# Two GNN layers over a binary adjacency: comparisons shared eight and eight, counts one chunk ahead, x first and in eighths

## What is computed

```python
def _L0_gnn_ref(h, adj, W, a, w_ih, w_hh, b_ih, b_hh):
    Wh = h @ W
    src = Wh @ a[:F_out]
    dst = Wh @ a[F_out:]
    e = jax.nn.leaky_relu(src + dst.T, ALPHA)
    att = jnp.where(adj > 0, e, NEG_INF)
    att = jax.nn.softmax(att, axis=1)
    h_prime = att @ Wh
    gi = h_prime @ w_ih.T + b_ih
    gh = h @ w_hh.T + b_hh
    r, z, n = ...            # sigmoid, sigmoid, tanh(i_n + r * h_n)
    return (1.0 - z) * n + z * h

def _L1_gnn_ref(x, adj_matrix, W, b):
    h = jnp.einsum('nd,ed->ne', x, W) + b
    return jnp.matmul(adj_matrix, h)

h = jnp.maximum(_layernorm(x, axis=-1), 0.0)
x = x + _L0_gnn_ref(h, adj, ...)
h = jnp.maximum(_layernorm(x, axis=-1), 0.0)
x = x + _L1_gnn_ref(h, adj, L1_gnn_W, L1_gnn_b)
```

## Time and profile before

| | us |
|---|---|
| median of three runs | 1727.31 (1723.8 to 1727.42) |
| the profiled execution | 1724.32 |
| its span | 1722.4 |

### The profile page before, as it was taken

One profiled execution on the slowest core, in us unless ns is written; L12 is line 12 of the kernel. 1 busy time (PEld: TensorE's weight loads), 2 busy tenths in 40 slices (PEclk: granted clock), 3 DMA queues, 4 the chain that ended last, 5 costly groups with the idle time before them and its releaser, 6 DMA issues.

```text
span 1722.4 us, 35016 instructions
## 1 busy us (share of the span) xinstructions
PE 1571.6 (91%) x13260; PEld 1341.9 (78%) x13260; DVE 1237.2 (72%) x2668; ACT 925.9 (54%) x1419; POOL 34.3 (2%) x57
## 2 busy tenths in 40 slices
PE   3468999999999999899998999999999999999998
PEld 3346777777877878787877887778788888888887
DVE  4898999999999999999999999999925000000000
ACT  4767777777867777776887777777600000000000
POOL 2000000000000000000000000000000000000000
PEclk9678999999999999999999999999999999999999
DMA  7448888887888878888788887888635444444430
GB/s 300 161 162 318 296 304 323 319 313 272 324 321 316 318 270 317 323 321 319 270 324 323 318 319 271 319 326 321 263 150 220 166 164 164 170 172 175 174 137 13
DMA packets 78594, 446.02 MB, mean 259 GB/s; under 512 B 8992, under 2 KB 38624, under 8 KB 57056
## 3 DMA queue, kind: packets, MB, share of 16 engines
q1 hardware_dynamic: 72512, 440.34, 68.3%
q10 hardware_dynamic: 6048, 5.25, 0.9%
HBM read 361.63 MB, written 83.92 MB: 259 GB/s over the span
## 4 chain that ended last, share of the span: by engine, by line
PE 41%; DVE 23%; DMA 14%; issue 12%; ACT 8%; DVEq 1%; ACTq 0%; SPq 0%
PE A L894 26%; DMA X<-in_adjb_dram 14%; PE A L811 11%; DVE M L596 6%; DVE Y L582 5%; DVE M L604 4%; ACT JK L429 3%; ACT M L419 3%; PE GP L834 1%; DVE AE L613 1%; DVE h2n L672 1%; DMA X<-in_L_gnn_a_dram 1%; ACT M L385 1%; PE GP L835 1%; DVE nm L619 1%
## 5 line engine op out<-in xcount | busy, mean ns | idle before, releaser
L811 PE MATMUL A<-TB,M 128*128 128x259 f16 x8192 | 959.1, 279 | 54.2 <-issue 32.4
L811 PEld LDWEIGHTS A<-TB,M 128*128 128x128 fp8e4 x8192 | 806.6, 99 | 195.9 <-issue 60.3
L429 ACT ACTIVATE JK<-X 128x4096 uint8<-128x4096 uint32 x124 | 447.3, 3607 | 1.4 <-DMA X<-in_adjb_dram 1.3
L596 DVE TENSOR_SCALAR M<-SB,nd 128x256 fp8e4<-128x256 f32 x1280 | 347.4, 346 | 4.9 <-issue 4.2
L419 ACT ACTIVATE M<-SB,dsteep 128x256 fp8e4<-128x256 f32 x768 | 319.4, 500 | 0.1
L582 DVE TENSOR_SCALAR Y<-X 128x4096 fp8e4<-128x4096 f32 x128 | 292.6, 2286 | 16.8 <-DMA X<-in_adjb_dram 16.5
L724 DVE SCALAR_TENSOR_TENSOR hp<-A,XT 128x256 f32<-128x256 f32 x32 | 13.6, 424 | 373.1 <-PE A L894 364.6
L894 PE MATMUL A<-WG,X 128*128 128x256 f16 x2048 | 225.5, 273 | 0.9 <-DVE WG L678 0.9
L894 PE MATMUL A<-WG,TB 128*128 128x256 f16 x2048 | 224.9, 273 | 0.0
L894 PEld LDWEIGHTS A<-WG,X 128*128 128x128 fp8e4 x2048 | 200.3, 98 | 24.2 <-DVE WG L678 1.1
L894 PEld LDWEIGHTS A<-WG,TB 128*128 128x128 fp8e4 x2048 | 200.4, 98 | 23.2
(11 more groups left out here) (128 smaller groups left out, 733.5 us busy)
## 6 DMA issues: line engine op xcount, KB each, us to landing
X<-in_adjb_dram SPq DMA_DIRECT2D x128, 2048.0 KB, 8.9
mask_bytes<-Y SPq DMA_DIRECT2D x128, 512.0 KB, 5.6
X<-mask_bytes SPq DMA_DIRECT2D x16, 2048.0 KB, 9.0
TB<-mask_bytes SPq DMA_DIRECT2D x16, 2048.0 KB, 9.3
M<-in_xb_dram SPq DMA_DIRECT2D x4, 1024.0 KB, 8.8
h_columns<-Y SPq DMA_DIRECT2D x16, 256.0 KB, 2.0
h_rows<-M SPq DMA_DIRECT2D x4, 1024.0 KB, 4.2
XT<-in_xb_dram SPq DMA_DIRECT2D x32, 128.0 KB, 8.4
```

What stands on the lines that cost most here:

```text
L429: nc.scalar.activation(to, X[c % 2][:, :].bitcast(u32), ACT.Sign, accum_out=nz[:, bass.ts(g, 1), c:c + 1].rearrange("p g c -> p (g c)")).t ...
L596: ins = nc.vector.tensor_scalar(rows(mask1(c), jj), SB[u][:, :], nd[:, j:j + 1], None, ALU.is_ge, saturate=False)
L811: ins = nc.tensor.matmul(A[t][m][:, 0:2 * TW + 1], rows((mask1, mask2)[m](c), jj)[:, t * P:(t + 1) * P], TB[:, c * JC + jj, m, 0:2 * TW + ...
```

## The change

Eight edits come together.

1. `sign_mask` takes eight tiles of a chunk and `compare` eight, in place of six and ten. In the first row block ScalarE takes all sixteen (`first_on_act`).
2. `count` runs one chunk ahead: after `sign_mask` of chunk c stands the count of chunk c + 1. In the first block it stands where it stood, and the block's end has one more.
3. x is loaded in eight pieces, and SP waits for the last of them before it asks for the first adjacency chunks.
4. The statistics are taken in eighths, one piece ahead of the normalisation. VectorE normalises six tiles of each eight (L541 of the new kernel), ScalarE two. The rectifier moves out of it, into the copy of the transposed tiles (`column`) and into the first operation of `updated`.
5. `features`, the copies into WG, moves from VectorE to ScalarE.
6. `ones_of` of the very first chunk moves ahead of the chain of small operations. The transposed tiles are staged in AE and Y[1], so that Y[0] is free for it.
7. Two one-element activations (Exp, Sigmoid) are put where their function tables should be loaded.
8. Buffers X1, XT, HS, HT become slices of one tile R; semaphores are merged (three `turn` into one, which nobody waits on).

```diff
-ON_ACT = 6
+ON_ACT = 8
+BY_DVE = 6
+        def first_on_act(g):
+            return 0 if isinstance(g, int) and g == 0 else JC - ON_ACT
...
-                for q in range(4):
-                    sp.dma_start(H[:, q * 16:(q + 1) * 16, :], xb[:, q * 16:(q + 1) * 16, :]).then_inc(p_x[q], 16)
+                for q in range(8):
+                    sp.dma_start(H[:, q * 8:(q + 1) * 8, :], xb[:, q * 8:(q + 1) * 8, :]).then_inc(p_x[q], 16)
+                sp.wait_ge(p_x[7], 16)
...
-                    nc.scalar.activation(hTq[k % 4], TP[k % 2][:, :], ACT.Copy).then_inc(p_ht, 1)
+                    nc.scalar.activation(hTq[k % 4], TP[k % 2][:, :], ACT.Relu).then_inc(p_ht, 1)
+
+                def features(k):
+                    for b in range(2):
+                        act.wait_ge(p_wh, 2 * k + b + 1)
+                        t = k * 4 + b * 2
+                        nc.scalar.activation(
+                            WG[:, t:t + 2, 0:F + 2],
+                            WB[(2 * k + b) % 4][:, 0:2 * (F + 2)].rearrange("p (t f) -> p t f", f=F + 2),
+                            ACT.Copy).then_inc(p_ev, 1)
...
+                deviation(0)
+                for q in range(8):
+                    if q < 7:
+                        deviation(q + 1)
+                    act.wait_ge(p_nm, q + 1)
+                    for t in range(q * 8 + BY_DVE, q * 8 + 8):
+                        ins = nc.scalar.activation(H[:, t, :], H[:, t, :], ACT.Identity, bias=nmx[:, t:t + 1],
+                                                   scale=rsx[:, t:t + 1])
+                    ins.then_inc(p_ha, 1)
+                    if q == 7:
+                        nc.scalar.activation(wsq[:, :], epst[:, :], ACT.Exp)
+                    column(2 * q)
                     if q > 0:
...
+                        features(2 * q - 1)
+                    column(2 * q + 1)
+                    features(2 * q)
+                features(15)
...
+                nc.scalar.activation(wsq[:, :], epst[:, :], ACT.Sigmoid)
...
-                    for jj in range(JC - ON_ACT, JC):
+                    for jj in range(first_on_act(g), JC):
...
-                            count(g, u, k, c)
+                            if isinstance(g, int) and g == 0:
+                                count(g, u, k, c)
+                            if c < CS - 1:
+                                if not (isinstance(g, int) and g == 0):
+                                    count(g, u, k, c + 1)
+                            elif not (isinstance(g, int) and g == NS - 1):
+                                count(g + 1, 1 - u, k + u, 0)
...
+                    for t in range(q * 8, q * 8 + BY_DVE):
+                        ins = nc.vector.tensor_scalar(H[:, t, :], H[:, t, :], mvx[:, t, 0:1], rsx[:, t:t + 1], ALU.subtract,
+                                                      ALU.mult)
...
-                    for jj in range(JC - ON_ACT):
+                    for jj in range(first_on_act(g)):
...
-                    nc.vector.tensor_tensor(x1v, HS[u][:, :].rearrange("p (t f) -> p t f", f=F), nn[:, :, :],
-                                            ALU.subtract).then_inc(d_u, 1)
+                    nc.vector.scalar_tensor_tensor(x1v, HS[u].rearrange("p (t f) -> p t f", f=F), 0.0, nn[:, :, :], ALU.max,
+                                                   ALU.subtract).then_inc(d_u, 1)
```

More of the change, by code:

```diff
@@ L80, in binary_adjacency @@
         JK = sb("JK", [P, 8 * TW])
[L81 to L84, removed]
+        R = sb("R", [P, 8, RW])
+        X1, XT, HS, HT = [[R[:, i, :], R[:, j, :]] for i, j in ((0, 1), (5, 2), (6, 3), (7, 4))]
         SB = [sb(f"SB{b}", [P, RW]) for b in range(2)]
@@ L185, in binary_adjacency @@
             sem(n) for n in ("c_y", "c_cnt", "c_ua", "c_ud", "c_m1", "c_m2", "c_pe"))
-        turn_a, turn_v, turn_p = sem("turn_a"), sem("turn_v"), sem("turn_p")
+        turn = sem("turn")
         s_in = [sem(f"s_in{b}") for b in range(2)]
@@ L495, in stats @@
                     dve.wait_ge(p_x[q], 16)
-                    for t in range(q * 16, q * 16 + 16):
+                    for t in range(q * 8, q * 8 + 8):
                         ins = nc.vector.bn_stats(stx[:, t, :], H[:, t, :])
@@ L535, in _, with ones_of @@
                         ins.then_inc(p_dg, 1)
-                features(3)
+                def ones_of(g, u, k, c):
+                    dve.wait_ge(c_in[c % 2], (k * 4 + u * 2 + c // 2 + 1) * 16)
+                    wait(dve, c_st[c % 2], (k * 4 + u * 2 + c // 2) * 16)
+                    wait(dve, c_m2, g * CS + c - 1)
+                    if isinstance(g, int) and g == 0 and c == 1:
+                        for b in range(2, 4):
+                            dve.wait_ge(p_htout[b], 64)
+                    dve.sem_inc(turn, 1)
+                    nc.vector.tensor_scalar(Y[c % 2][:, :].bitcast(f8), X[c % 2][:, :], 1.0, MARK, ALU.is_equal, ALU.mult,
+                                            saturate=False).then_inc(c_y, 1)
+                ones_of(0, 0, 0, 0)
                 dve.wait_ge(p_ev, 32)
@@ L600, in combine @@
                 def combine(g, c):
-                    dve.wait_ge(c_ud, g * CS + c + 1)
+                    wait(dve, c_ud, (g - 1) * CS + c + 1)
                     dve.wait_ge(c_ua, g * CS + c + 1)
@@ L640, in updated @@
                 def updated(q, u, n):
-                    x1 = X1[u][:, :]
+                    x1 = X1[u]
                     x1v = x1.rearrange("p (t f) -> p t f", f=F)
@@ L878, in slot @@
                                 wait(pe, e_ev[t], g)
-                            pe.sem_inc(turn_p, 1)
+                            pe.sem_inc(turn, 1)
                             ins = products(g, c, t)
```

148 lines of the change are left out of this document (62 added, 86 removed).

## The result

| | before | after |
|---|---|---|
| median us | 1725.55 (1723.53 to 1727.42) | 1659.03 (1656.96 to 1660.3) |
| the profiled execution's span | 1722.4 | 1655.0 |
| gates of the second block | 202.81 | 198.91 |
| a turn of the loop (29 of them) | 36.00 | 33.81 |

The account below looks back on a forecast made before the run. VectorE was taken to set the 36.0 us turn; with the change the ring of ScalarE and PE at 33.8, plus half of 0.7 for the clock, gives 34.1. Gains of 1.8 + 29 x 1.9 make 1670 us, range 1654 to 1709.

Parts of the forecast that it names:

- the clock: In the loop, PE partly at the lower clock level: half of 0.7 us a turn added; lower bound none, fewer gaps.
- the start: Up to the second block's gates: WG at 53.0, gates at 201.0 against 202.81, a gain of 1.8 us.
- The ring of ScalarE and PE: In the loop: ScalarE's gates to evacuation, 15.1 us, plus PE's first chunk to next gates, 18.65; 33.8 us sets the turn.
- The count ahead: In the loop: adjacency buffers are free about a chunk earlier, so 0.6 us of waiting go; least room 1.7 us.
- the same comes out the other way: Cross-check of the loop's turn: 36.0 us less VectorE's saving of 2.2 is 33.8.
- The wait for hp: On PE in each block: the 1.6 us wait goes, one of about 1 us for the evacuation comes.
- SP's new wait: Behind chunk 3's load SP waits about 2 us for the new x of two blocks ago; costed at nothing.
- The elementwise rule: Skill rule sending plain elementwise work to VectorE; by it alone the loop would be 1.0 us a turn longer.
- Rival 3: In the loop: VectorE's saving turns into a wait of the same size, no gain, 1727 us; chance 0.05.
- Rival 2: In the loop: adjacency loads fall behind and stop PE; if 16 us each, turn 36.6, 1745 us; chance 0.07.
- The tail to WG: In the start: the way through PE and ScalarE to WG, with a table load, 4.7 us (3 to 6).
- The sum: Whole kernel: 1.8 + 29 x 1.9 = 56.9 us gained, profiled execution 1667.4, median 3.0 above it, 1670 us.

Follow-up runs that it names:

- late_count: The changed kernel with the count of a chunk back behind its own chunk's comparisons, the split still eight and eight; 1710.33 us, turn 35.52 us.
- old_loop_new_start: The changed kernel with six comparisons on ScalarE, ten on VectorE, and the count behind its own chunk's comparisons; 1719.51 us, turn 36.05 us.
- split6: The changed kernel with ScalarE back at six comparisons and VectorE at ten from the second block on, count still ahead; 1707.24 us, turn 35.54 us.
- split7: The changed kernel with seven comparisons on ScalarE and nine on VectorE from the second block on; 1675.27 us, turn 34.46 us.
- first_even: The changed kernel with the first block's comparisons shared eight and eight instead of all sixteen on ScalarE; 1651.37 us.
- pool_later: The changed kernel with GpSimd's work on the biases held back until VectorE has normalised its last tile; 1660.05 us.
- pool_x1_later: The changed kernel with GpSimd's bias work held back and the second adjacency chunk's load moved behind the tenth store of transposed features; 1656.74 us.
- all_three_x1_last: The kernel all_three with the second adjacency chunk asked for behind the last store of transposed features; 1617.16 us.
- all_three: The changed kernel with evacuation in halves around the count, nine comparisons on ScalarE, and an evenly shared first block; 1616.03 us.

## Why the prediction was right, point by point

The mechanism and its parts came out as forecast; two terms were mis-sized, the clock and the start.

- **What bounds the loop.** Right. The ring of ScalarE and PE was put at 15.1 + 18.65 = 33.8 and came out at 15.11 + 18.65 = 33.76; the mean turn is 33.81. (Its 7.16 us for a chunk isn't a third of the 192 products, which is 7.21, but what a further chunk adds, 14.48 - 7.32; measured the same way it holds.) VectorE at 33.2 showed as the next one: 33.40 once the ring was shorter, and one more comparison on it gave 34.46. PE at 32.8 was the last, and came out at 32.77.
- **The count ahead removes the 0.6 us of waiting.** Right, and too modest. It was costed as 0.6; with the split alone the late count eats all but 0.5 of VectorE's 2.2. The two are one edit in effect. That "the same comes out the other way", 36.0 less 2.2, was chance: with VectorE's 2.2 alone taken off, `late_count` stood at 35.5.
- **The wait for hp goes, one of 1 us for the evacuation comes.** Right, 0.9 us measured.
- **SP's new wait costs nothing.** Right, 1.7 us each.
- **The clock, +0.35 us a turn.** Wrong, and the largest miss of the sum, 29 x 0.35 = 10 us. I took half of what the stretch lost before; the loss was nought, the granted clock 1.00. The lower bound, "none of it (fewer gaps)", was the true value. What the old loop's slow chunks hang on stays open. In the kernel before, two turns have the same two waits and different chunks behind them:

```profile
369.25 0.44 PE L842 MATMUL TG<-ident,h2n 128*128 128x128 f32 x2 [0.58 <-DVE h2n L672]
371.32 0.44 PE L820 MATMUL TG<-ident,hp 128*128 128x128 f32 x2 [1.63 <-DVE hp L629]
371.60 7.32 PE L811 MATMUL A<-TB,M 128*128 128x259 f16 x64
...
405.40 0.44 PE L842 MATMUL TG<-ident,h2n 128*128 128x128 f32 x2 [0.57 <-DVE h2n L672]
407.47 0.44 PE L820 MATMUL TG<-ident,hp 128*128 128x128 f32 x2 [1.63 <-DVE hp L629]
407.74 8.97 PE L811 MATMUL A<-TB,M 128*128 128x259 f16 x64
```

  In `old_loop_new_start` such slow chunks are back (clock 0.98). In `late_count`, with waits for hp of up to 1.6 us in every turn, and in `split6` the clock between 600 and 1100 us was 1.00, though earlier in `late_count` a chunk behind one took 8.97 as well (at 329.01). So neither wait by itself decides it. "TensorE: Matmul & The Clock Gate" of the Trainium skill, section "The HAM clock gate", has the low level as the resting state that activity lifts; the changed loop, whose PE went from 546 to 564 busy us and from 0.98 to 1.00, agrees. A fuller PE isn't the whole of it, though: PE is busy 466 of 500 us in `late_count` and 468 in `split6`, at 1.00, and 470 in the kernel before, its slow chunks counted in, at 0.98.
- **The elementwise rule.** By "ScalarE: Activation LUTs" of the Trainium skill, section "Rules for kernel authors", the split would have cost. The price it goes by is real, 3.29 us for eight here against VectorE's 2.18. It decides nothing while the dearer engine has room: `split6`, which follows it, is 48 us slower. Rival 3, in which the loop gains nothing, is out.
- **Rival 2, late loads.** Out, by little: a load took 9.3 us from issue to landing in the median and 10.7 at most in the loop (180 to 1160 us). The load with the least room, chunk 3's, is asked for at 612.65 in the turn shown and wanted at 623.43, 10.8 us later: 1.5 us of room in the median, forecast 1.7, and next to none for the slowest. With fewer comparisons on ScalarE (`split6`, `split7`) the counts do wait for loads, up to 2.2 us, but there they are not on the path.
- **The start, gain of 1.8 us.** It was 3.9, and that this is near is in part luck; the sum of its terms hid larger misses. VectorE began its statistics at 10.99 instead of 15.6, since the weights' product, for which it waits first, came at 10.9. (That the adjacency loads, now issued at 16.95, no longer share the queues with the weights would explain it; it wasn't tried.) It then lost 3.8 us beside GpSimd. It finished normalising at 45.8, forecast 48.3. The tail to WG took 6.6 us instead of 4.7, and 6 was my bound: ScalarE still had two tiles to normalise, a table load of 1.28 us and the last copies. WG was read at 52.32, forecast 53.0. The next terms held: 2.4 to the table (forecast 2.9), chunks 17.19 apart (17.3, in which sixteen comparisons and the hand-over should read 6.47, not 6.45), PE's first chunk at 72.63 (73.4), the second block's first chunk at 145.26 (146.5), 2.1 us slower than a full one (2.6). The edits of the start weren't run one by one, so what each is worth isn't shown. Together they are worth more than 3.9: with the first block shared evenly (`first_even`) the first gates are 5.6 us ahead of the kernel before (158.58 against 164.14) and the second block's 10.5.
- **The sum.** Forecast for the profiled execution 1667.4, measured 1656.96 (its span 1655.0). Of the 10.4 us the loop, where only the clock term missed, is 8.4 (29 x (34.1 - 33.81)), and the start 2.1. The median lies 2.1 us above the profiled execution, where 3.0 were taken.

## What to carry to other kernels

Sum each engine's turn, and then each ring that leads through two engines' orders, in which the work that happens to stand ahead of a hand-over counts in full. The highest of these sums is the turn; the distance to the second highest is all that an edit to the first can win, so the edits have to be weighed as a set: two worth 0.5 us a turn each were worth 2.2 together. When the ring leads, move the hand-over ahead of work that nobody waits for (3.6 us out of the ring at no cost elsewhere), and only then shift work between engines.

## What was not expected of the hardware

- VectorE's 128x128 fp32 normalisations took up to 1556 ns instead of 340 while GpSimd ran its own 128x640 fp32 operations, and GpSimd's 128x256 addition took 2.63 us instead of 0.73 beside VectorE's conversion of the adjacency. "GPSIMD Engine Reference" of the Trainium skill, section "Specifications", has the two engines share their SBUF interfaces, with contention for VectorE's instructions in a two-port mode or with two SBUF inputs. The trace agrees that they contend; in which mode these instructions ran no row tells. GpSimd's share of the span is 2%, and it cost VectorE 3.8 us in the start; holding it back only moved the clash (`pool_later`).
- A small store issued behind two large loads waits for them. The transposed features' first stores, asked for at 17.80 behind two loads of 2 MB at 16.95, held ScalarE for 3.4 us until 31.10 (7.3 in `pool_later`). With one load ahead of them ScalarE was released at 27.50 (`pool_x1_later`), and with the second load moved behind the last store the wait was gone (`all_three_x1_last`). In `all_three` such a wait of 4.8 us cost nothing, since VectorE was the slower of the two.
